# A conditional linear with eight LoRA experts: two passes, and block products in Strassen's form

## The reference, cut to what matters

```python
# x: (64, 64, 1024)   itok: (64,)   cond_weights: (16, 64, 64)
# W_org: (1024, 1024)  lora_down: (8, 1024, 64)  lora_up: (8, 64, 1024)
W = cond_weights[itok]
y = einsum('bct,bcd->bdt', x, W)                  # a 64x64 matrix for each batch
base = einsum('bsi,oi->bso', y, W_org)            # K = 1024
q = einsum('bi,ki->bk', y.mean(axis=1), Wq)
coeffs = softmax(einsum('bk,ek->be', q, lora_keys) / sqrt(128))
h = einsum('bsi,eir->bser', y, lora_down)         # K = 1024, 512 columns
delta = einsum('be,bser,ero->bso', coeffs, h, lora_up)   # K = 512
out = x + base + delta
```

## Time and profile before

| | us |
|---|---|
| median of 3 runs | 813.61 |
| lowest, highest | 812.59, 813.75 |
| the profiled execution: its span, first to last instruction | 811.1 |
| PE busy in it | 795.6 (98%) |
| DVE, ACT, POOL busy | 373.8, 207.8, 11.9 |

### The profile page before, as it was taken

One profiled execution on the slowest core, in us unless ns is written; L12 is line 12 of the kernel. 1 busy time (PEld: TensorE's weight loads), 2 busy tenths in 40 slices (PEclk: granted clock), 3 DMA queues, 4 the chain that ended last, 5 costly groups with the idle time before them and its releaser, 6 DMA issues.

```text
span 811.1 us, 10497 instructions
## 1 busy us (share of the span) xinstructions
PE 795.6 (98%) x3825; PEld 668.7 (82%) x3825; DVE 373.8 (46%) x758; ACT 207.8 (26%) x346; POOL 11.9 (1%) x12
## 2 busy tenths in 40 slices
PE   5989999999999999999999999999999999999998
PEld 5878888888888888888888888888888888888886
DVE  5655444535444535444535444535444535444531
ACT  5532222212222212222212222212222212222210
POOL 3020000000000000000000000000000000000000
PEclk9999999999999999999999999999999999999999
DMA  8510111110111110111110111110111110111100
GB/s 295 201 54 15 54 53 40 53 53 14 53 53 40 53 52 14 53 53 40 53 52 14 53 53 40 53 52 14 53 53 40 53 53 14 53 53 40 53 27 26
DMA packets 21930, 43.63 MB, mean 54 GB/s; under 512 B 6938, under 2 KB 6946, under 8 KB 21922
## 3 DMA queue, kind: packets, MB, share of 16 engines
q1 hardware_dynamic: 21906, 43.53, 15.6%
q10 hardware_dynamic: 16, 0.00, 0.0%
HBM read 26.74 MB, written 16.78 MB: 54 GB/s over the span
## 4 chain that ended last, share of the span: by engine, by line
PE 98%; DVE 1%; ACT 0%; DMA 0%; issue 0%; SPq 0%; DVEq 0%
PE o_ps L590 43%; PE h_ps L581 22%; PE o_ps L609 21%; PE y_ps L566 8%; PE gt_ps L597 2%; PE y_ps L654 1%; PE s_ps L669 0%; DMA x_sb<-in_x_dram 0%; PE gt_ps L654 0%; PE t_ps L654 0%; DVE y_full L407 0%; DVE up_l L493 0%; ACT y_part L302 0%; DVE x_l L395 0%; ACT x_h L295 0%
## 5 line engine op out<-in xcount | busy, mean ns | idle before, releaser
L590 PE MATMUL o_ps<-org_t_h,y_h 128*128 128x512 f32 x512 | 203.5, 397 | 0.0
L590 PE MATMUL o_ps<-org_t_h,y_l 128*128 128x512 f32 x512 | 200.1, 391 | 0.0
L590 PE MATMUL o_ps<-org_t_l,y_h 128*128 128x512 f32 x512 | 199.8, 390 | 0.0
L470 DVE TENSOR_TENSOR out_sb<-o_ps,x_sb 128x512 f32<-128x512 f32 x64 | 44.3, 692 | 192.2 <-PE o_ps L609 192.1
L590 PEld LDWEIGHTS o_ps<-org_t_l,y_h 128*128 128x128 f32 x512 | 96.2, 188 | 21.0
L590 PEld LDWEIGHTS o_ps<-org_t_h,y_h 128*128 128x128 f32 x512 | 96.4, 188 | 17.2
L590 PEld LDWEIGHTS o_ps<-org_t_h,y_l 128*128 128x128 f32 x512 | 96.5, 189 | 16.7
L581 PE MATMUL h_ps<-down_h,y_h 128*128 128x512 f32 x256 | 103.2, 403 | 0.0
L295 ACT ACTIVATE x_h<-x_sb 128x512 fp32r<-128x512 f32 x64 | 72.4, 1180 | 117.4 <-DMA x_sb<-in_x_dram 117.4
L609 PE MATMUL o_ps<-up_h,gt_h 128*128 128x512 f32 x256 | 99.8, 390 | 2.5 <-DVE up_l L493 1.3
L581 PE MATMUL h_ps<-down_h,y_l 128*128 128x512 f32 x256 | 100.3, 392 | 0.0
(11 more groups left out here) (70 smaller groups left out, 683.9 us busy)
## 6 DMA issues: line engine op xcount, KB each, us to landing
x_sb<-in_x_dram SPq DMA_DIRECT2D x32, 512.0 KB, 3.6
out_dram<-out_sb SPq DMA_DIRECT2D x64, 256.0 KB, 2.0
stage_sb<-in_L_ffn_W_org_dram SPq DMA_DIRECT2D x5, 512.0 KB, 4.2
stage_sb<-in_L_ffn_lora_down_dram SPq DMA_DIRECT2D x4, 512.0 KB, 4.7
out_sb<-in_L_ffn_W_org_dram SPq DMA_DIRECT2D x3, 512.0 KB, 7.4
stage_sb<-in_L_ffn_lora_up_dram SPq DMA_DIRECT2D x3, 512.0 KB, 4.2
cw_sb<-in_L_cond_weights_dram SPq DMA_DIRECT2D x64, 16.0 KB, 2.3
stage_sb<-in_L_ffn_Wq_dram SPq DMA_DIRECT2D x1, 512.0 KB, 6.6
```

The lines of the kernel that those rows point to most:

```text
L470: nc.vector.tensor_tensor(out_sb[:, p, cols], o_ps[:, h, :], x_sb[:, p, cols], ALU.add).then_inc(out_ready, 1)
L590: nc.tensor.matmul(o_ps[:, h, :], y[s][:, p, k, :], org_t[m][:, k, h * BANK:(h + 1) * BANK], start=(k == 0 and q == 0), stop=False)
```

## The change

The kernel makes two passes over the batches and keeps y, and the sum of x's share and the rest, in DRAM between them.

First pass, in eight groups of four tiles. h is now made transposed (`lora_down` is the stationary operand, y of four tiles the 512 moving columns), so no transposes of g are left, and one router step serves four tiles. A group is two pairs of tiles. A pair's LoRA product (256 rows, K = 512, 1024 columns) is cut in 2x2 blocks and done as seven block products in Winograd's form of Strassen's algorithm: 7 x 2 chunks x 3 passes = 42 matmuls, for 48. The block sums of g (`sum_1` to `sum_4`), their high parts (ACT) and low parts (DVE) and the combinations of the products (`take_r` on ACT, `end_c..` on DVE) are new. Each y goes to `y_dram` and each LoRA result to `r_dram`. The y of the next group is made between the products of this one; its low part and the low part of x are made by POOL.

Second pass, in 16 pairs: y, r and x are loaded again, POOL adds r and x, and base is done as seven block products of 4 chunks x 3 passes, 84 matmuls for 96. In between stands a step of its own: `W_org` is turned (`turn_org`, among the last products of pass one), summed in blocks and split in seven pairs of high and low parts.

The loops are unrolled. All the orders are written out anew.

```diff
-            def tile(t, p, last=False):
-                make_h(t, p, range(KC))
-                rest(t, p, last)
...
+            def up_product(j, n, bank, first, built):
+                pe.wait_ge(ga_hi[n], j + 1)
+                pe.wait_ge(ga_lo[n], j + 1)
...
+                for e in range(2):
+                    for i, (s, w) in enumerate(PASSES):
+                        mm = nc.tensor.matmul(bank, ga[s][:, n, e, :], tu[w][:, n, e, :],
...
+            def make_y(n):
+                t, r = n // 2, n % 2
...
+                if n >= 8:
+                    pe.wait_ge(y_added, n)
...
+                                              chunk_cols(xs[s][:, p, :], 4 * r + k),
...
+            for q in range(NQ):                      # PE; n = 8 * (q + 1), "more": all but the last q
+                make_h(q, 0)
+                make_scores(q)
+                make_h(q, 1)
+                make_h(q, 2)
+                make_h(q, 3)
+                up_1(j0)
+                    make_y(n)
+                up_2(j0)
+                    make_y(n + 1)
+                up_6(j0)
+                up_7(j0)
+                    make_y(n + 2)
+                up_5(j0)
+                    make_y(n + 3)
+                up_1(j1)
+                up_3(j0)
+                    make_y(n + 4)
+                up_4(j0)
+                    make_y(n + 5)
+                up_2(j1)
...
+                    load_x(t)                        # SP; t = 4 * (q + 1)
+                    load_x(t + 1)
+                    store_y(n)
+                    store_r(j0, 0, c11_ready)
+                    store_y(n + 1)
+                    load_x(t + 2)
+                    store_y(n + 2)
+                    store_r(j0, 3, c22_ready)
+                    store_y(n + 3)
+                    load_x(t + 3)
...
+                    copy_y(n + 2)                    # ACT
+                    split_x(t + 2)
...
+                    add_y(n + 1)                     # DVE
+                    split_cw(t + 2)
+                lo_block(j1, P1, 0, 0)
+                    add_y(n + 2)
...
+                    add_y(n + 3)
+                    split_cw(t + 3)
+                lo_sum(j1, P6, 1)
+                lo_sum(j1, P7, 2)
+                sum_4(j1)
+                    add_y(n + 4)
...
+            sp.wait_ge(tb_hi, NS)                    # SP, between the passes
+            sp.wait_ge(tb_lo, NS)
+            load_r(0)
+            load_yb(1)
+            load_r(1)
```

More of the change, by code:

```diff
@@ L12 @@
 AX = mybir.AxisListType
+PASSES = ((0, 0), (1, 0), (0, 1))
+P1, P2, P6, P7, P5, P3, P4 = range(7)
+NS = 7
 def adaln_ffn(
@@ L92, in adaln_ffn @@
[L92 to L101, removed]
@@ L117, in adaln_ffn @@
[L117 to L125, removed]
-        turn_ps = [gt_ps[:, :], t_ps[:, :]] + [
-            y_ps[:, j * YC // 2:(j + 1) * YC // 2, :, :].rearrange("p k h n -> p (k h n)") for j in range(2)]
@@ L363, in _ @@
+            split_y(5)
+            copy_y(6)
+            copy_y(7)
             act.wait_ge(ones_ready, 1)
-            nc.scalar.activation(ones_r[:, :], ones[:, :], ACT.Copy).then_inc(ones_copied, 1)
+            copy(ones_r[:, :], ones[:, :], ones_copied)
+            split_y(6)
+            split_y(7)
             split_z(0)
-            split_org(0)
-            split_org(1)
-            exps(0)
-            for n in range(2, OC):
-                split_org(n)
-            split_x(1, 1, 0)
@@ L541, in _ @@
-            add_x(0, 0, 0)
-            add_x(0, 0, 1)
-            softmax(1)
-            tile(1, 1, 1)
-            with dve.Fori(0, T // 2 - 1 - 1) as i:
-                for u in range(2):
-                    tile(2 * i + (2 + u), u, i + 1 + u, free=i + 1)
-            tile(T - 2, 0, T // 2 - 1, free=T // 2 - 1)
-            tile(T - 1, 1, T // 2, last=True, free=T // 2 - 1)
+            split_up(P3, 3)
+            dve.wait_ge(tu_lo, 1)
+            sub(U11, U12, U11, tu_sum)
+            scale_h(0, 0)
@@ new lines, in base_product @@
+            def base_product(p, n, bank, first, built):
+                pe.wait_ge(ba_hi[n], p + 1)
+                pe.wait_ge(ba_lo[n], p + 1)
+                if p == 0:
+                    pe.wait_ge(tb_hi, built)
+                    pe.wait_ge(tb_lo, built)
+                for k in range(4):
+                    for i, (s, w) in enumerate(PASSES):
+                        mm = nc.tensor.matmul(bank, ba[s][n][:, k, :], tb[w][n][:, k, :],
+                                              start=(first and k == 0 and i == 0), stop=(k == 3 and i == 2),
+                                              skip_group_check=True)
+                mm.then_inc(base_done[n], 1)
@@ L691, in _ @@
-            pe.wait_ge(org_hi, 2 * OC)
-            pe.wait_ge(org_lo, 2 * OC)
-            turn_g(0)
-            base(0, 0, 1, range(HK))
-            make_y(1, 0)
-            base(0, 0, 1, range(HK, KC))
-            pe.wait_ge(y_added, YR + 1)
-            make_y(1, 1)
-            add_lora(0, 0, first=True)
-            add_lora(0, 1)
-            make_scores(1)
-            with pe.Fori(0, T // 2 - 1) as i:
-                for u in range(2):
-                    tile(2 * i + (1 + u), (1 + u) % 2)
```

1348 lines of the change are left out of this document (949 added, 399 removed).

## The result

| | us |
|---|---|
| before, median beside it | 813.7 (812.6 to 814.0) |
| the changed kernel, median of 4 runs | 1124.6 (1122.7 to 1128.3) |
| ratio | 1.384, interval 1.381 to 1.387 |
| forecast | 912, range 855 to 960 |

The account below looks back on a forecast made before the run. PE bounds the kernel: 698.6 us of work + 108 group waits + 21 clock + 2 + 36 between passes + 15 second pass + 2 + 23 start + 2 + 3 = 910.6, plus 2.5 = 913, stated as 912; range 855 to 960.

Parts of the forecast that it names:

- Second pass: Base products in 16 pairs: PE work 19.1 us a pair, plus 1 us of waiting each, 15 in all.
- DMA moves 4.2 MB a pair, 220 GB/s, half of 415: Second pass: a pair's transfers need only half the 415 GB/s of the earlier trace's busiest stretch.
- the range of 0 to 45: Second pass: bounds in us on PE's waiting over all pairs, put at 15.
- One thing can be ruled out early: make_y: reading stationary x with a stride of eight elements costs nothing extra; its matmuls stay at 0.119 us.
- Waits in a group: First pass: PE waits 15.4 us in each of seven groups, 108 in all, mainly two waits of 6.4 and 7.5.
- the walk's 9.0 us: First-pass group: time from the second y half's addition to the third's, traced through the queues; PE waits 6.4 of it.
- SP issues its load only behind the store: First-pass group: the third tile's x load waits for the second y half's store; 0.45 plus 3.7 us of the chain.
- the covers hold: Rival: x loads come early enough that PE does not stop for them in the groups; 795 us, chance 0.11.
- The port: First-pass groups: DVE's cws low part waits for POOL's 2.4 us x low part; rival without this 876 us, chance 0.12.
- The clock: First-pass groups: PE's clock falls after long waits, 3 us a group, 21 in all; rival without this 892, chance 0.15.
- Between the passes: From the last group's h to the third base product: PE waits 36 us of 41.8, kept within 30 to 45.
- start: First make_h at 31 us, before 18.75; 23 us added (18 to 30), plus 2 for cold matmuls.

Follow-up runs that it names:

- e12: Changed kernel with only the second pass's x and out DRAM views made 128 straight rows, not 4 groups of 32 (result not the layer's): 932.1 us.
- e3: Changed kernel with all four x loads of a group issued ahead of its first store of y: 1119.6 us.
- e14: e10 with the cws low part on POOL instead of the later place on DVE, and the second pass's first r and x loads issued earlier: 856.1 us.
- e13: Changed kernel with each second-pass out store and x load issued as four DMAs, 32 rows outermost, same bytes and addresses: 945.3 us.
- e16: Changed kernel with each second-pass out store and x load issued as two DMAs, 2 groups of 32 rows outermost: 1426.7 us.
- e6: Changed kernel with a pair's row halves as its two tiles (933.1 us), plus y_dram padding so y moves in 512-byte pieces: 939.3 us.
- e5: The kernel before, with x parts written straight and make_y's stationary operand read with a stride of eight elements: 866.8 us.
- e10: Changed kernel with row halves as tiles, a group's x loads first, third and fourth tiles' cws low part later on DVE, x in chunk order: 879.9 us.

## Why the prediction was wrong

**Second pass, the failed step.** "DMA moves 4.2 MB a pair, 220 GB/s, half of 415": the step took the rate of the earlier trace rows, from transfers with 128 partitions outermost, for transfers that are written with 4 outermost. Priced by the form, with the 90 GB/s of the trace after, it is 31 us a pair and not 20, and 16 x 10.8 = 173 us are missing. The mechanism, that DMA is hidden behind PE, was wrong as well: DMA and SP's queue became the bound. With the views straight (e12) the pass takes 312.9 us from the third base product; the forecast has 319.7. So the rest of this term held, within 2%, and the range of 0 to 45 bounded only the engines, not the transfers. The rule of the Trainium skill named above stood against this change and was not weighed.

**"One thing can be ruled out early", failed.** It carried the 0.10 us of strided transposes over to matmuls with a 256-column moving operand in the other kind. They cost 0.242 in place of 0.119, seven of each eight: 8 halves x 0.87 = 7.0 us in each group. The transposes were no bound for this form, and the nearest rows of the same kind had no strided one; a range up to twice the price was due.

**Waits in a group, right in place, a third too long, and one link slack.** Forecast 13.9 for the two; PE waited 65.5 us for `y_full` in seven groups, 9.4 each:

```profile
L1115 PE MATMUL y_ps<-cws,x_h 128*128 128x256 f32 x236 | 96.2, 408 | 70.8 <-DVE y_full L711 65.5
```

```profile
361.78 0.48 PE L1115 MATMUL y_ps<-cws,x_h 128*128 128x256 f32 x1 [4.49 <-DVE y_full L711]
...
375.72 0.48 PE L1115 MATMUL y_ps<-cws,x_h 128*128 128x256 f32 x1 [4.81 <-DVE y_full L711]
```

The places are those foretold, and the walk's 9.0 us between the additions is 8.9 (`y_full` of the second half ends at 352.7, of the third at 361.6). The waits are shorter since PE's y work in between is twice as long, by the step above: 7.0 more work and 4.5 less waiting make 2.5 of the 2.8 us by which a group is longer. So the sum of a group came out within 3 us by two errors that cancel, which is luck. The link "SP issues its load only behind the store" was slack here. I had counted 0.45 + 3.7 for it, and ACT's own queue, behind the longer y half, ended at the same moment; e3 showed that. With a y half at the foreseen 0.95 us the load might have been the limit; no run has that alone. The rival "the covers hold" (795) rested on early x loads, and e3 has them at 5 us less.

**The port, right in kind.** `cws` takes 1516 ns in the mean where the earlier trace rows have 283, and 2.33 beside a POOL operation of 2.34. Its worth is about 11 us, a difference of two single runs, not 27.

**The clock, right in kind.** Granted clock behind the waits of 4.5 and 4.8 us:

```profile
360.00:364.00 4.00, 2.22 (x9) 2.25 (x10) 3.93 (x7) 0.63 (x1) 1.82 (x2) 0.81 0.22 84
...
376.00:380.00 4.00, 4.00 (x15) 3.52 (x16) 2.53 (x6) 2.06 (x5) 1.45 (x1) 0.57 0.35 131
```

0.57 of full speed is near the lower level, 1.2 GHz. What it costs in the groups, 21 us in the forecast, no run shows by itself. In the second pass it falls too, behind the long wait of a pair (0.52 and 0.50 at 806 to 814), and adds to the cost of the slow transfers: 1320 matmuls took 337 us of busy time there, and 307 in e12. These 30 us and the 147.9 of waiting are nearly all of the 180 by which this pass is longer than in e12.

**Between the passes, start.** 13 us too low: the first x loads of the second pass have the 4 x 32 form. From the issue of the first r load to POOL's addition it is 19.9 us (607.99 to 627.92), where 7.5 were forecast, and 8.6 in e12, where this stretch is within 2 us of the forecast. The start of 38.9 in place of 31 has several parts. Ahead of the third tile's x stand 3.5 MB of weights, not 3; this x was there at 21.3, where the forecast has 18.5. Behind it the trace has 16 matmuls for the router's keys that the forecast leaves out (28.28 to 31.98), and y halves of about 2 us at a granted clock of 0.58 to 0.71. How much each weighs is not shown, and e14's start, with chunk order, is no earlier (41.5).

Put together, e12 has a span of 930.3 and the sum was 910.6: start 8, groups 17, the rest -5. So the forecast fits a kernel whose x and `out` transfers use all DMA engines, in part by the errors that cancel in a group.

## What to carry over

Before you divide bytes by a rate, look at the outermost dimension of each access pattern of a DMA: a rate holds only for the form it was read from, and a busy share that sits at a quarter while a transfer is waited for says that a quarter of the engines works on it (here 0.25 with 4 outermost, 0.13 with 2). A wait in an in-order queue costs whatever stands behind it, so move the waiting instruction before you shorten what it waits for. And price an operand's form (stride, kind) by a row of the same form, or keep twice the price in the range.

## What the runs showed of the hardware

- Same bytes and addresses, outermost dimension 32, 4 and 2 (e13, the changed kernel, e16): 945, 1125 and 1427 us. Such transfers also hold SP: two y loads took 9.4 us to issue behind them, and 1.2 behind straight ones (e12). What holds SP there, a full queue being my guess, is not shown.
- 512-byte pieces in DRAM, twice the packets (112,089 for 58,841), cost about 6 us of 933 in one run (e6).
- A float32r stationary operand of 128 columns with a stride of 8 elements takes 332 ns to load instead of 194, and 256-column matmuls then start 0.242 us apart instead of 0.119 (e5 and the kernel before). Float32 transposes with the same stride ran at 0.10.
- A 128x1024 operation that puts x in chunk order, and so reads x with a stride of 8 elements: POOL's subtraction takes 3.09 us in the mean (e10) against 2.37 straight (the changed kernel), ACT's copy 2.17 against 1.06.
